# A six-layer transformer kernel on one Trainium2 core: closing tile, first steps of a layer and opening tile in another order, and the exponential's table loaded at another place

## The chip, the cores and the metric

One Trainium2 chip, one of its NeuronCores. The core has five engines that run their own instruction streams and meet at semaphores: TensorE (PE, matmuls and transposes), VectorE (DVE), ScalarE (ACT), GpSimd (POOL) and SyncE (SP, which issues the DMAs here). The metric is the device time of one execution in microseconds; less is better.

## The reference, cut to what matters

```python
x = x + layernorm(attn(layernorm(x)))          # x: (2, 1024, 128)
h = layernorm(x)
for i in range(6):                             # DEPTH
    h = attn_layer(h, Wqkv[i], ...) + h        # 16 heads of 64, window 32
    h = ffn_layer(h, ln_g[i], ...) + h
x = x + layernorm(h)

def attn_layer(x, Wqkv, qs, ksc, Wo):
    q, k, v = split(x @ Wqkv)                  # 128 -> 3 * 1024
    q, k = l2norm(q) * qs, l2norm(k) * ksc     # per head
    q, k = rotary(q), rotary(k)
    sim = q @ k.T * 8, masked to 32 keys back
    return (softmax(sim) @ v) @ Wo

def ffn_layer(x, g, bln, W1, b1, W2, b2):
    xn = layernorm(x) * g + bln
    a, gate = split(xn @ W1 + b1)              # 128 -> 2 * 341
    return a * gelu(gate) @ W2 + b2
```

In each layer half of the channels are taken from the row before (a token shift) ahead of both parts. All is float32.

## The kernel before

The 2048 rows are 16 tiles of 128 rows. All activations stay in the core's memory, channels on the partitions (`xA` ahead of attention, `xB` between attention and feed-forward). A first, small attention fills the first 180 us; then come six layers. A layer has 16 attention tiles, one by one, and a feed-forward part over four groups (s = 0 to 3) of four tiles each. The code of layer 0 and of layer 5 is written out; layers 1 to 4 are one loop over the layer on each engine. Within a layer the tiles 0 and 1 are written out, tiles 2 to 13 are a loop of two tiles per turn, then tiles 14 and 15. Tile 0 is called *opening*, tile 15 *closing*. The order of the work on each engine is written out by hand; semaphores alone hold the engines together.

One tile t of attention does this, while tile t+1 is being prepared:

- Preparation: ScalarE copies the input (`copy_input`), VectorE makes its rest (`input_rest`), TensorE projects six blocks of 512 columns (`project` x = 0 to 5; x = 0, 1, 2, 4 are queries and keys, x = 3, 5 values). For each of the four query and key blocks ScalarE squares (`square`, L519), VectorE reduces the squares and multiplies by the rotary tables (`rotary`, L808 to L818), and GpSimd does the rotation's rest (`rotate`: a power L329, a sum L331, a product L334 that gives `w_nat`). TensorE transposes `w_nat` (`transpose_heads`, L1208), ScalarE copies it to `qT` or `kT` (`heads_T`, L541), and values go out by `values` (L526), which lets the SP queue store them in the layout that the last matmul wants (`move_values`).
- Attention for heads 0 to 7 and then 8 to 15: `scores` (L1158, the mask, and L1167), `maxima` on VectorE (L765), `exps` on ScalarE (L503, two groups of four heads), `transpose_probs` (L1174), `probs_out` (L512), `weigh_values` (L1187), `heads_out` on VectorE (L773, L775, which gives `o_nat`), `transpose_out` (L1214), `heads_out_T` (L532), `project_out` (L1222) and `residual` (L782, L783).

The closing tile has no tile t+1 to prepare; in its place the feed-forward part begins: `shifted(s)` on ScalarE (L464, L465), `transpose_in(s)` on TensorE (L1271), `norm_stats(s)` on VectorE (L924 to L930), a power on GpSimd (L405), `norm(s)` on VectorE (L938), `transpose_normed(s)` (L1278), `normed_T(s)` on ScalarE (L644). For each group s there are three chunks i: `gate_up(s, i)` (L1290, L1292), `gate(s, i)` on ScalarE (the Gelu, L653), `hidden(s, i)` on VectorE (L949); then `down(s)` (L1303) and `output(s)` on VectorE (L957, L959). `split` and `rest` make the next layer's weights ready meanwhile. From s = 2 on, the next layer's tile 0 is prepared between the groups, in numbered parts `start(..., part)`.

Exp and Gelu are in different tables of ScalarE: a load of the Gelu table stands ahead of each layer's first Gelu, one of the exponential's table ahead of the first `exps` of layers 1 to 5.

The lines that two of the prediction's steps hang on are these (VectorE's closing tile, ScalarE's tile):

```python
maxima(t, p, 0)
if closing:
    norm_stats(0)
if not opening:
    heads_out(t - 1, 1 - p, 1)
...
exps(t, p, 0, 0)
if not closing:
    square(t + 1, 0)
```

Of the kernel before, what the change touches and what calls it, by code (L numbers as in the profile page):

```python
# [34 lines left out]
def build(nc, x, Wa, ba, Wp, bp, Wqkv, Wo, scales, W1, W2, par, rope, ident, identb, mask, select, out):  # L35
# [3 lines left out]
    with ctx:  # L39
# [87 lines left out]
        veps = sb("veps", [P, TILES])  # L127
        rstd = sb("rstd", [P, TILES])
# [294 lines left out]
        def _(eng):  # L423
# [155 lines left out]
            def start(t0, part):  # L579
# [7 lines left out]
                if part == 2:  # L587
                    square(t0, 2, True)
                    values(t0, 0, 0)
                if part == 3:  # L590
                    heads_T(t0, 0, 0, 6)
                    square(t0, 3, True)
                    heads_T(t0, 0, 1, 4)
                    values(t0, 0, 1)

            def layer(l, last):
                t0 = l * TILES

                def tile(t, n, p, opening, closing):
                    if closing:  # L600
                        shifted(l, 0)
                        shifted(l, 1)
                    exps(t, p, 0, 0)
                    if not closing:
                        square(t + 1, 0)
                    heads_T(t, p, 2, 6 if opening else 4)
                    if not opening:
                        heads_out_T(t - 1, 1, 6)
                    exps(t, p, 0, 1)
                    if not closing:  # L610
                        square(t + 1, 1)
                    heads_T(t, p, 3, 4)
                    if not closing and not (isinstance(n, int) and n == TILES - 2):
                        copy_input(n + 2, p)
                    probs_out(t, 0, 0, 6)
                    if not closing:
                        square(t + 1, 2)
                    probs_out(t, 0, 1, 4)
# [42 lines left out]
                for s in range(SUPERS):  # L661
# [5 lines left out]
                    gate(s, 1)  # L667
                    if s == 0 and not last:
# [14 lines left out]
                if not last:  # L683
                    start(t0 + TILES, 3)
            for part in range(4):
# [12 lines left out]
        def _(eng):  # L698
# [217 lines left out]
            def layer(l, last):  # L916
# [45 lines left out]
                def tile(t, n, p, opening, closing):  # L962
                    maxima(t, p, 0)
                    if closing:
                        norm_stats(0)
# [4 lines left out]
                    if closing:  # L970
                        norm(0)
# [26 lines left out]
                for s in range(SUPERS):  # L998
                    hidden(s, 1)
# [4 lines left out]
                    elif not last:  # L1004
                        start(l + 1, 3)
# [36 lines left out]
        def _(eng):  # L1042
# [202 lines left out]
            def start(l, part):  # L1245
# [7 lines left out]
                if part == 1:  # L1253
                    project(t0, 0, 2, True)
                    project(t0, 0, 3, True)
                if part == 2:
                    transpose_heads(t0, 0, 6)
                    project(t0, 0, 4, True)
                if part == 3:
# [3 lines left out]
            def layer(l, last):  # L1263
# [42 lines left out]
                def tile(t, n, p, opening, closing):  # L1306
# [19 lines left out]
                    if closing:  # L1326
                        transpose_in(1)
                    else:
                        project(t + 1, 1 - p, 1)
                    eng.wait_ge(tp_free, t * 4 + (2 if opening else 3))  # L1330
                    transpose_heads(t, 3, 4)
                    if opening:
                        eng.wait_ge(tp_free, t * 4 + 3)
                    else:
                        eng.wait_ge(ot_evac, t * 2)
                    transpose_probs(t, 0, 0, 6)
# [138 lines left out]
```

## Time and profile before

| | us |
|---|---|
| median of 3 runs | 2061.19 (2056.7 to 2067.75) |
| the profiled execution | 2066.27 |
| its span, first to last instruction | 2064.5 |
| TensorE busy | 1912.5 (93%) |
| GpSimd busy | 1669.6 (81%) |
| ScalarE busy | 1596.2 (77%) |
| VectorE busy | 1556.0 (75%) |
| mean granted TensorE clock | 0.972 |

Busy time is the time in which an engine has an instruction in work. The granted clock is a share of TensorE's full speed: 1.00 is 2.4 GHz, 0.50 is 1.2 GHz. The time outside the span, 1.8 us, is start and end of the program.

### The profile page before, as it was taken

The page shows a single profiled execution, that of the slowest core. Times are in us where ns is not written, and L with a number is a line of the kernel's source. Part 1 is how long each engine was busy: PE and PEld are TensorE (multiplying, and loading weights), DVE is VectorE, ACT ScalarE, POOL GpSimd, SP SyncE. Part 2 cuts the span into 40 slices and gives each one's busy share as a digit, 9 for nine tenths or more (in the row PEclk, how much of TensorE's full clock was granted, in tenths as well). Part 3 has the DMA queues.
Part 4 walks back from the last instruction along what each step waited for, and adds up shares of the span by engine and source line. Part 5 has one row for each costly group of instructions (what it writes and reads, how often), then busy time and mean ns, then how long its engine had stood idle before and what let it go on. Part 6 is the DMA issues. An engine that isn't in the chain of part 4 may idle for free.

```text
span 2064.5 us, 67226 instructions
## 1 busy us (share of the span) xinstructions
PE 1912.5 (93%) x22192; PEld 1452.2 (70%) x22192; DVE 1556.0 (75%) x4021; ACT 1596.2 (77%) x5607; POOL 1669.6 (81%) x1264
## 2 busy tenths in 40 slices
PE   6996999988999988999988999988999989999997
PEld 4664777765777764777764777774777774777773
DVE  5786888866888866888866788865788876788876
ACT  5874888875888874888874888884888875888873
POOL 3335999976999975999975999984999985999971
PEclk8997999999999999999999999999999999999999
DMA  3001211111211112122112111212211111111210
GB/s 117 14 12 49 60 48 46 46 42 60 60 48 46 46 42 61 48 50 56 46 36 67 48 46 49 56 35 63 56 46 46 46 47 35 50 46 46 50 41 21
DMA packets 44547, 99.42 MB, mean 48 GB/s; under 512 B 7345, under 2 KB 24209, under 8 KB 43505
## 3 DMA queue, kind: packets, MB, share of 16 engines
q1 hardware_dynamic: 44400, 97.59, 18.1%
q8 instruction: 78, 1.28, 0.3%
q14 instruction: 69, 0.56, 0.1%
HBM read 19.59 MB, written 1.05 MB: 10 GB/s over the span
## 4 chain that ended last, share of the span: by engine, by line
PE 81%; ACT 7%; issue 6%; DVE 4%; POOL 1%; DMA 0%; SPq 0%; DVEq 0%; ACTq 0%; POOLq 0%
PE bank L1174 10%; PE bank L1187 9%; PE bank L1222 8%; PE bank L1201 8%; PE bank L1167 7%; PE bank L1203 6%; PE bank L1202 6%; PE bank L1208 6%; PE bank L1158 3%; ACT kT L541 3%; PE bank L1292 3%; PE bank L1290 3%; PE bank L1303 2%; PE bank L1214 2%; ACT prob L503 2%
## 5 line engine op out<-in xcount | busy, mean ns | idle before, releaser
L329 POOL TENSOR_TENSOR rn<-n2c,half_neg 128x8 f32<-128x8 f32 x384 | 636.5, 1658 | 117.9 <-DVE n2c L815 116.8
L503 ACT ACTIVATE prob<-bank,nmax 128x96 f32<-128x96 f32 x1536 | 502.6, 352 | 134.9 <-DVE nmax L765 134.7
L331 POOL TENSOR_TENSOR tsum<-tc_,ts_ 128x512 f32<-128x512 f32 x384 | 489.7, 1275 | 0.0
L334 POOL TENSOR_TENSOR w_nat<-tsum,rn 128x512 f32<-128x512 f32 x384 | 400.9, 1044 | 37.7 <-POOL tsum L331 15.1
L808 DVE TENSOR_REDUCE n<-nat 128x8 f32<-128x512 f32 x384 | 262.2, 683 | 158.4 <-ACT nat L519 143.6
L503 ACT ACTIVATION_READ_ACCUMULATOR prob<-bank,nmax 128x1 f32 x1536 | 333.0, 217 | 0.0
L765 DVE TENSOR_REDUCE nmax<-bank 128x4 f32<-128x384 f32 x384 | 196.2, 552 | 162.4 <-PE bank L1167 162.4
L1201 PE MATMUL bank<-w_hi,xs 128*128 128x512 f32 x576 | 277.9, 482 | 20.1 <-DVE ts_ L818 17.5
L1174 PE MATMUL bank<-idf,prob 128*96 128x128 f32 x1536 | 247.3, 285 | 53.0 <-ACT kT L541 29.1
L512 ACT ACTIVATE pT<-bank 96x512 f32<-96x512 f32 x384 | 230.6, 600 | 74.7 <-PE bank L1174 72.5
L818 DVE TENSOR_TENSOR ts_<-bank,ropeL 128x256 f32<-128x256 f32 x768 | 285.9, 414 | 0.0
L519 ACT ACTIVATE nat<-bank 128x512 f32<-128x512 f32 x384 | 232.9, 607 | 42.3 <-PE bank L1203 33.6
L811 DVE TENSOR_TENSOR tc_<-bank,ropeL 128x512 f32<-128x512 f32 x384 | 261.2, 680 | 0.0
L1174 PEld LDWEIGHTS bank<-idf,prob 128*96 128x96 f32 x1536 | 160.0, 128 | 116.5 <-ACT kT L541 81.0
L1208 PE MATMUL bank<-idf,w_nat 128*128 128x128 f32 x1536 | 236.8, 277 | 3.4 <-POOL w_nat L334 3.2
L1208 PEld LDWEIGHTS bank<-idf,w_nat 128*128 128x128 f32 x1536 | 181.5, 141 | 77.6 <-issue 29.1
L1203 PE MATMUL bank<-w_hi,xs_lo 128*128 128x512 f32 x576 | 229.4, 398 | 0.0
L1202 PE MATMUL bank<-w_lo,xs 128*128 128x512 f32 x576 | 229.4, 398 | 0.0
L1187 PE MATMUL bank<-vspace,pT 96*64 96x64 f32 x6144 | 221.2, 225 | 0.0
L1187 PEld LDWEIGHTS bank<-vspace,pT 96*64 96x64 f32 x6144 | 194.7, 138 | 31.4 <-issue 20.7
L1222 PE MATMUL bank<-oT,wo 128*128 128x128 f32 x1536 | 207.5, 279 | 4.1 <-ACT oT L532 4.1
L1222 PEld LDWEIGHTS bank<-oT,wo 128*128 128x128 f32 x1536 | 190.0, 195 | 6.0 <-ACT oT L532 5.5
(124 smaller groups left out, 3328.1 us busy)
## 6 DMA issues: line engine op xcount, KB each, us to landing
vspace<-v_nat SPq DMA_DIRECT2D x96, 384.0 KB, 4.0
vspace<-v_nat SPq DMA_DIRECT2D x96, 256.0 KB, 3.4
vspace<-v_nat SPq DMA_DIRECT2D x95, 128.0 KB, 2.2
nat<-w_qkv SPq DMA_DIRECT2D x5, 1536.0 KB, 7.9
wo<-w_o SPq DMA_DIRECT2D x6, 512.0 KB, 4.0
w<-w SPq DMA_DIRECT2D x6, 341.0 KB, 3.1
shared<-w_qkv SPq DMA_DIRECT2D x1, 1536.0 KB, 9.9
w<-w SPq DMA_DIRECT2D x6, 192.0 KB, 3.2
```

The lines of the kernel that those rows point to most:

```text
L329: nc.gpsimd.tensor_tensor(rn[:, r, :], n2c[:, r, :], half_neg[:, 0:8], ALU.pow).then_inc(pool_step, 1)
L331: nc.gpsimd.tensor_tensor(tsum[:, r, :], tc_[:, r, :], ts_[:, r, :], ALU.add).then_inc(pool_step, 1)
L334: nc.gpsimd.tensor_tensor(w_nat[:, r, :].rearrange("p (h d) -> p h d", d=D), tsum[:, r, :].rearrange("p (h d) -> p h d", d=D), rn[:, r, :] ...
L503: last = nc.scalar.activation(prob[:, 4 * b + i, :], SB[b][:, i * SPAN:(i + 1) * SPAN], ACT.Exp, bias=nmax[:, p, 8 * G + 4 * b + i:8 * G + ...
L818: last = nc.vector.tensor_tensor(ts_[:, r, :].rearrange(heads3, d=D)[:, :, lo:lo + D // 2], pj[:, :].rearrange(heads3, d=D)[:, :, hi:hi + ...
L1174: last = nc.tensor.transpose(RING[at][0:SPAN, i * P:(i + 1) * P], prob[:, 4 * b + i, :], idf[:, :])
L1187: last = nc.tensor.matmul(OB[qs, a:a + D], pT[:, 4 * b + i, qs], vw[:, p, half, head * D:(head + 1) * D], start=True, stop=True, skip_grou ...
L1201: nc.tensor.matmul(PJ[x % 2][:, :], xs[:, p, :], hi, start=True, stop=False)
L1202: nc.tensor.matmul(PJ[x % 2][:, :], xs[:, p, :], rest, start=False, stop=False)
L1203: nc.tensor.matmul(PJ[x % 2][:, :], xs_lo[:, p, :], hi, start=False, stop=True).then_inc(pj_ready, 1)
L1208: last = nc.tensor.transpose(RING[at][:, i * P:(i + 1) * P], w_nat[:, j % 2, i * P:(i + 1) * P], idf[:, :])
L1222: last = nc.tensor.matmul(YB[:, 0:P], wo[:, 4 * G + i, :], oT[:, G, i * P:(i + 1) * P], start=G == 0 and i == 0, stop=G == 1 and i == 3)
```

## The change

ScalarE: in the closing tile `shifted(1)` moves behind `heads_out_T`, and the two `probs_out` of heads 0 to 7 move ahead of `heads_T` 3. In the opening tile `square(t + 1, 0)` moves ahead of the first `exps`. In the feed-forward part the value copy of tile 0 moves behind `gate(3, 1)`, and a one-column Exp is put behind the last Gelu, ahead of the last part of `start`. VectorE: in the closing tile `norm_stats(0)` moves behind `heads_out` and `residual`; rotary 2 of the next layer's tile 0 moves ahead of `hidden(3, 1)`. TensorE: in the closing tile `transpose_probs` of heads 0 to 7 come ahead of `transpose_heads` 3 (banks 4 and 6 change places), and `project_out(t - 1, 1)` comes ahead of `transpose_probs` 1,0; `project` 3 of the next layer's tile 0 moves behind `gate_up(3, 1)`.

```diff
@@ ScalarE, def start(t0, part)
                 if part == 2:
                     square(t0, 2, True)
+                if part == 3:
                     values(t0, 0, 0)
-                if part == 3:
+                if part == 4:
                     heads_T(t0, 0, 0, 6)
@@ ScalarE, def tile
                     if closing:
                         shifted(l, 0)
-                        shifted(l, 1)
+                    if opening:
+                        square(t + 1, 0)
                     exps(t, p, 0, 0)
-                    if not closing:
+                    if not opening and not closing:
                         square(t + 1, 0)
                     heads_T(t, p, 2, 6 if opening else 4)
                     if not opening:
                         heads_out_T(t - 1, 1, 6)
+                    if closing:
+                        shifted(l, 1)
                     exps(t, p, 0, 1)
                     if not closing:
                         square(t + 1, 1)
+                    if closing:
+                        probs_out(t, 0, 0, 4)
+                        probs_out(t, 0, 1, 6)
                     heads_T(t, p, 3, 4)
...
-                    probs_out(t, 0, 0, 6)
                     if not closing:
+                        probs_out(t, 0, 0, 6)
                         square(t + 1, 2)
-                    probs_out(t, 0, 1, 4)
+                        probs_out(t, 0, 1, 4)
@@ ScalarE, def layer
                     gate(s, 1)
+                    if s == 3 and not last:
+                        start(t0 + TILES, 3)
...
                 if not last:
-                    start(t0 + TILES, 3)
+
+                    nc.scalar.activation(one_exp[:, :], half_neg[:, 0:1], ACT.Exp)
+                    start(t0 + TILES, 4)
@@ VectorE, def tile
                     maxima(t, p, 0)
-                    if closing:
-                        norm_stats(0)
                     if not opening:
                         heads_out(t - 1, 1 - p, 1)
                         if not (isinstance(n, int) and n == 1):
                             residual(t - 2, n - 2)
                     if closing:
+                        norm_stats(0)
                         norm(0)
                         norm_stats(1)
@@ VectorE, feed-forward
                 for s in range(SUPERS):
+                    if s == 3 and not last:
+                        start(l + 1, 3)
                     hidden(s, 1)
                     if s + 2 < SUPERS:
                         norm_stats(s + 2)
                     elif s == 2 and not last:
                         start(l + 1, 0)
-                    elif not last:
-                        start(l + 1, 3)
@@ TensorE, def start
                 if part == 1:
                     project(t0, 0, 2, True)
+                if part == 2:
                     project(t0, 0, 3, True)
-                if part == 2:
+                if part == 3:
                     transpose_heads(t0, 0, 6)
                     project(t0, 0, 4, True)
-                if part == 3:
+                if part == 4:
                     transpose_heads(t0, 1, 4)
                     project(t0, 0, 5, True)
@@ TensorE, def tile
                     if closing:
+
                         transpose_in(1)
+                        eng.wait_ge(tp_free, t * 4 + 3)
+                        transpose_probs(t, 0, 0, 4)
+                        eng.wait_ge(ot_evac, t * 2)
+                        transpose_probs(t, 0, 1, 6)
+                        eng.wait_ge(pt_evac, t * 4 + 1)
+                        transpose_heads(t, 3, 4)
...
                     if closing:
+                        eng.wait_ge(pt_evac, t * 4 + 2)
                         transpose_normed(0)
+                        weigh_values(t, p, 0)
+                        project_out(t - 1, 1)
+                        eng.wait_ge(tp_free, t * 4 + 4)
+                        transpose_probs(t, 1, 0, 4)
@@ TensorE, feed-forward
                     if s + 2 < SUPERS:
                         transpose_in(s + 2)
+                    elif s == 3 and not last:
+                        start(l + 1, 2)
...
                     gate_up(s, 2)
                     if s == 3 and not last:
-                        start(l + 1, 2)
+                        start(l + 1, 3)
...
                 if not last:
-                    start(l + 1, 3)
+                    start(l + 1, 4)
```

## Rows read from the trace of the kernel before

**Rows 1.** The page, part 1: busy us, share of the span, instructions.

```profile
PE 1912.5 (93%) x22192; PEld 1452.2 (70%) x22192; DVE 1556.0 (75%) x4021; ACT 1596.2 (77%) x5607; POOL 1669.6 (81%) x1264
```

**Rows 2.** Windows, steady stretches: window, us, busy us (instructions), granted clock, DMA share, GB/s.

```profile
206.35:438.86 232.51, 224.81 (x2960) 182.19 (x2957) 190.06 (x474) 201.72 (x713) 225.01 (x173) 1.00 0.21 51
...
sum 1394.75, PE 1349.58 PEld 1092.87 DVE 1139.68 ACT 1209.96 POOL 1341.75; mean PE 224.93 PEld 182.14 DVE 189.95 ACT 201.66 POOL 223.63
```

**Rows 3.** Windows, closings of layers 0 and 2, and the sum of six.

```profile
438.86:457.45 18.59, 15.57 (x171) 12.32 (x171) 8.24 (x31) 12.07 (x38) 11.29 (x6) 0.91 0.01 2
...
1062.98:1080.36 17.38, 14.09 (x171) 10.96 (x171) 8.24 (x31) 11.82 (x38) 11.29 (x7) 1.00 0.00 1
...
sum 112.85, PE 93.95 PEld 74.93 DVE 49.46 ACT 71.92 POOL 58.45; mean PE 15.66 PEld 12.49 DVE 8.24 ACT 11.99 POOL 9.74
```

**Rows 4.** Windows, feed-forward parts of layers 0 to 4: their sum.

```profile
sum 133.67, PE 132.98 PEld 65.91 DVE 87.00 ACT 75.01 POOL 45.47; mean PE 26.60 PEld 13.18 DVE 17.40 ACT 15.00 POOL 9.09
```

**Rows 5.** Windows, openings of layers 0, 1, 2 and 5, and the sum of six.

```profile
180.20:206.35 26.15, 20.88 (x175) 14.23 (x175) 19.03 (x45) 15.82 (x53) 25.34 (x20) 0.84 0.31 96
484.24:516.22 31.98, 25.88 (x191) 16.42 (x190) 21.42 (x54) 18.47 (x56) 26.75 (x21) 0.95 0.31 97
795.11:830.33 35.22, 26.98 (x191) 17.04 (x190) 21.40 (x54) 18.83 (x56) 27.33 (x21) 0.90 0.29 89
...
1735.45:1765.84 30.39, 25.92 (x192) 16.42 (x191) 21.40 (x54) 18.58 (x56) 26.90 (x21) 0.94 0.17 45
sum 196.02, PE 153.78 PEld 98.79 DVE 126.02 ACT 109.33 POOL 160.96; mean PE 25.63 PEld 16.47 DVE 21.00 ACT 18.22 POOL 26.83
```

**Rows 6.** Timeline of TensorE in the closings: start, us, what [idle before <-releaser].

```profile
439.86 0.63 PE L1214 MATMUL bank<-idf,o_nat 128*128 128x128 f32 x4 [2.92 <-DVE o_nat L775]
...
444.66 0.49 PE L1158 MATMUL bank<-msk,idb 128*128 128x384 bf16 x2
...
1067.49 0.49 PE L1158 MATMUL bank<-msk,idb 128*128 128x384 bf16 x2
```

**Rows 7.** Timeline of ScalarE, first copy of the closing tile of layer 0.

```profile
434.46 0.62 ACT L464 ACTIVATE shared<-xB 64x512 f32<-64x512 f32 x1
```

**Rows 8.** Timeline of TensorE, end of the feed-forward part and opening, layer 1.

```profile
487.56 0.47 PE L1201 MATMUL bank<-w_hi,xs 128*128 128x512 f32 x1 [1.52 <-DVE ts_ L818]
...
493.14 0.47 PE L1201 MATMUL bank<-w_hi,xs 128*128 128x512 f32 x1 [0.78 <-DVE ts_ L818]
...
499.20 0.50 PE L1201 MATMUL bank<-w_hi,xs 128*128 128x512 f32 x1
```

**Rows 9.** Timeline of ScalarE, opening tiles of layers 0, 1 and 2.

```profile
192.97 0.34 ACT L503 ACTIVATE prob<-bank,nmax 128x96 f32<-128x96 f32 x1 [2.08 <-DVE nmax L765]
...
194.25 0.61 ACT L519 ACTIVATE nat<-bank 128x512 f32<-128x512 f32 x1
...
200.24 0.34 ACT L503 ACTIVATE prob<-bank,nmax 128x96 f32<-128x96 f32 x1 [0.56 <-DVE nmax L765]
...
499.99 1.28 ACT L503 ACT_TABLE_LOAD   x1 [1.57 <-DVE nmax L765]
...
502.56 0.61 ACT L519 ACTIVATE nat<-bank 128x512 f32<-128x512 f32 x1
...
808.58 0.60 ACT L526 ACTIVATE v_nat<-bank 128x512 f32<-128x512 f32 x1
812.72 1.28 ACT L503 ACT_TABLE_LOAD   x1 [3.54 <-issue]
...
816.13 0.60 ACT L519 ACTIVATE nat<-bank 128x512 f32<-128x512 f32 x1 [0.72 <-issue]
```

**Rows 10.** Timeline of GpSimd, last product of tile 0 and first power of tile 1, layer 1.

```profile
499.33 1.04 POOL L334 TENSOR_TENSOR w_nat<-tsum,rn 128x512 f32<-128x512 f32 x1
504.75 1.65 POOL L329 TENSOR_TENSOR rn<-n2c,half_neg 128x8 f32<-128x8 f32 x1 [4.38 <-DVE n2c L815]
```

**Rows 11.** Windows, a stretch of the opening tile of layer 4.

```profile
1441.32:1451.32 10.00, 6.42 (x47) 4.51 (x48) 4.67 (x12) 5.94 (x20) 5.80 (x5) 0.50 0.49 175
```

More of the change, by code:

```diff
@@ L127, in build @@
         veps = sb("veps", [P, TILES])
+        one_exp = sb("one_exp", [P, 1])
         rstd = sb("rstd", [P, TILES])
@@ L683, in layer @@
                 if not last:
-                    start(t0 + TILES, 3)
-            for part in range(4):
+                    nc.scalar.activation(one_exp[:, :], half_neg[:, 0:1], ACT.Exp)
+                    start(t0 + TILES, 4)
+            for part in range(5):
                 start(0, part)
@@ L1327, in tile @@
                         transpose_in(1)
+                        eng.wait_ge(tp_free, t * 4 + 3)
[4 more added lines that the diff above has]
+                        transpose_heads(t, 3, 4)
                     else:
                         project(t + 1, 1 - p, 1)
[L1330 to L1336, printed above, removed]
-                    if not closing:
+                        eng.wait_ge(tp_free, t * 4 + (2 if opening else 3))
+                        transpose_heads(t, 3, 4)
+                        if opening:
+                            eng.wait_ge(tp_free, t * 4 + 3)
+                        else:
+                            eng.wait_ge(ot_evac, t * 2)
+                        transpose_probs(t, 0, 0, 6)
                         project(t + 1, 1 - p, 2)
-                    eng.wait_ge(tp_free, t * 4 + 4)
-                    transpose_probs(t, 0, 1, 4)
+                        eng.wait_ge(tp_free, t * 4 + 4)
+                        transpose_probs(t, 0, 1, 4)
                     scores(t, n, p, 1)
@@ L1344, in tile @@
                         project(t + 1, 1 - p, 3)
-                    eng.wait_ge(pt_evac, t * 4 + 1)
                     if closing:
+                        eng.wait_ge(pt_evac, t * 4 + 2)
                         transpose_normed(0)
+                        weigh_values(t, p, 0)
+                        project_out(t - 1, 1)
+                        eng.wait_ge(tp_free, t * 4 + 4)
+                        transpose_probs(t, 1, 0, 4)
                     else:
+                        eng.wait_ge(pt_evac, t * 4 + 1)
                         transpose_heads(t + 1, 0, 6)
-                    weigh_values(t, p, 0)
-                    eng.wait_ge(pt_evac, t * 4 + 2)
-                    transpose_probs(t, 1, 0, 4)
-                    if not opening:
-                        project_out(t - 1, 1)
+                        weigh_values(t, p, 0)
+                        eng.wait_ge(pt_evac, t * 4 + 2)
+                        transpose_probs(t, 1, 0, 4)
+                        if not opening:
+                            project_out(t - 1, 1)
                     if closing:
@@ L1400, in layer @@
                 if not last:
-                    start(l + 1, 3)
-            for part in range(4):
+                    start(l + 1, 4)
+            for part in range(5):
                 start(0, part)
```

## The prediction

> **What bounds the kernel now.** I read the page first. TensorE is busy 93% of the span, which looks like the bound, but GpSimd is at 81% and ScalarE at 77% [rows 1]. So I cut each layer with the windows view into four stretches whose ends I took from the timelines. (1) Steady: from the first scores of tile 1 to the end of the last `w_nat` multiply of tile 15. All six are 232.5 us on average; GpSimd is busy 225.01 of 232.51 us in the first, at full granted clock: that stretch runs at the rotation's pace, and no edit is in it [rows 2]. (2) Closing: from that multiply to the last half of `project_out`. It takes 17.38 us in layer 2, where the granted clock stayed at 1.00 (the higher level, 2.4 GHz), 18.59 us in layer 0, where it was 0.91, and 112.85 us in all six [rows 3]; the five others so lost 8.6 us against layer 2, 1.7 each. (3) Feed-forward: from there to the first rotation of the next layer, 133.67 us in five, 26.73 each; TensorE is busy 132.98 of it, so it is TensorE's [rows 4]. (4) Opening: from that rotation to the first scores of tile 1. 26.15 us in layer 0, 31.98 in layer 1, 35.22 in layer 2, 30.39 in layer 5, 196.02 in all, so 72.28 for layers 3 and 4 [rows 5]. The reader is to see that layer 0 does this work, without a table load and without a feed-forward part beside it, in 4 to 10 us less than the others. Closing and opening are the only places where an edit can pay.
>
> **Closing tile.** TensorE waits 2.92 us for `o_nat`, because VectorE does `norm_stats(0)` ahead of `heads_out`; behind it stand the output transpose, the projection and all else of the tile [rows 6]. The swap on VectorE takes this wait away: the o_nat multiply, which needed only `weigh_values`, comes about 2.9 us earlier. But that isn't the gain, since ScalarE ends last next. Its new order from 434.46 [rows 7] is `shifted(0)` (two copies, 1.30), four exps (1.28, the distance of the rows at 192.97 and 194.25 in layer 0), two head copies (1.0), `shifted(1)` (1.30), four exps (1.28): 440.6. Then three handoffs of about 0.15, a transpose of probabilities (0.45), one of keys (0.60), the copy between them hidden, `heads_T` 3 (0.60) and the wait of `scores`: second scores at 443.0, which is 4.15 us after the last multiply at 438.86. Before, it is at 444.66 (5.80) in layer 0, where the clock had fallen, and 4.51 (1067.49 less 1062.98) in layer 2, where it hadn't [rows 6]. From there to the end the same chain follows. So a closing at full clock should take 17.38 - 0.37 = 17.0. What the clock does is the unknown. Before, TensorE's 2.92 us of idleness is followed by a fallen clock in layer 0 and, by the sum of times, in the four others too. In the new order TensorE still idles some 2.9 us, in pieces of at most 1.3, while ScalarE works. If the clock stays up everywhere: 112.85 - 6 x 17.0 = 10.9 us gained; if it falls as before: 6 x 0.37 = 2.2 us. I take the middle, 6.5.
>
> **End of the feed-forward part.** `project` 3 goes behind `gate_up(3,1)`, and rotary 2 ahead of `hidden(3,1)`. TensorE's waits of 1.52 us (for rotary 1) and 0.78 us (for rotary 2) [rows 8] are covered: the first by 1.7 us of gate_up, the second because rotary 2 no longer waits for hidden(3,1), and starts when GpSimd has finished rotation 0. `down(3)` then waits some 0.25 us for hidden(3,2), which is behind rotary 2. So all behind it comes 1.52 + 0.78 - 0.25 = 2.05 us earlier: the first scores, and `project(t+1,0)` from 499.20 to 497.15. The new load and the one-column Exp stand behind the last Gelu, where ScalarE waits for TensorE anyway; 1.28 us plus some 0.3 end about as square 3 becomes ready. Without that cover they would cost 1.6 per layer in layers 1 to 5. The value copy triggers the SP queue's three stores of values 2 us earlier; nothing asks for them before `weigh_values`, behind the second scores. The window to the first rotation keeps its 26.7.
>
> **Opening tile, layers 1 and 5.** Before, `square(t+1,0)` starts at 502.56: behind the scores' maxima, the load (1.28) and four exps [rows 9]. First in line, it starts when its projection ends, 497.15 + 1.0 = 498.15, 4.4 us earlier. GpSimd then is free only at 499.33 + 1.04 = 500.4, so rotation (1,0) starts at 500.5 instead of 504.75: 4.25 us [rows 10]. How fast the rest follows layer 0 tells: from its first exps at 192.97 to the third group at 200.24 are 7.27 us, with square and all, and from there to its end (180.20 + 26.15 = 206.35) 6.11 [rows 5, 9]. 498.15 + 7.27 + 6.11 = 511.5, instead of 484.24 + 31.98 = 516.22: a window of 27.3, gain 4.7. Layer 5 goes from 30.39 to 27.3: 3.1. Layer 0 has no load to save and its GpSimd is busy 25.34 of 26.15 us: square waits for its projection there, exps behind it: 0, within 0.3.
>
> The table load as the row has it: 1.28 us, and from its start to the square 2.57 us, all of it load and exps [rows 9]. The Trainium skill, page ScalarE: Activation LUTs, section What ACT_TABLE_LOAD costs, gives some 1283 ns plus a drain of 1380; by it another 1.4 us would leave the path in layers 1 and 5, 2.8 in sum. The trace has no room for that drain here, and I don't count it.
>
> **Opening tile, layers 2 to 4.** Here the table load isn't what ends last. The layers' loop jumps back, and ScalarE waits for nothing that the profile shows ("issue") for 3.54 us before the load and 0.72 us before the square [rows 9]; layers 1 and 5, entered without the jump, have no such wait. In layer 2 the last value copy ends at 808.58 + 0.60 = 809.18, the second wait 6.95 us later at 816.13, and the window 14.2 us after that. The load passes within the 6.95 and saves nothing. I expect both waits to follow the value copy as before, 2.05 us earlier, and the square (0.5) to be done by the second: 2.6 us each, 7.8 in three. The Trainium skill, Runtime: NRT & Kernel Launch, section Instruction fetch mechanics, speaks against the change here: a taken branch to outside the two resident pages forces a fetch before work goes on, whatever the order behind it. The trace agrees, with the 3.54.
> Bounds: nothing but the square (0.5 each, 1.5), if the second fetch comes no earlier; and above, the 14.2 shrinks to layer 0's 206.35 - 194.25 = 12.1, if TensorE's clock stays up: 6.3 more in three. I take the same 14.2, since TensorE still stands behind ScalarE's waits there.
>
> **Sum.** 6.5 (closings) + 4.7 + 3.1 + 7.8 = 22.1 us. The profiled execution took 2066.27 us, 1.8 around its span of 2064.5, and is 5.1 above the median of the three runs. It becomes 2044.2; the median 2061.2 becomes 2039.
>
> **Rivals.**
> - Handed to the clock and the fetch: closings 2.2, layers 2 to 4 1.5, and layers 1 and 5 lose 1.3 each to a fall of the clock like today's (7.8 - 2.6 = 5.2). 8.9 us, 2052. For it: the clock fell in most closings, and TensorE's idleness is only cut up. Against: the waits of 2 us and more go. 0.2.
> - The clock stays up: 10.9 + 7.8 + 7.8 + 6.3 = 32.8, 2028.4. For it: layer 2's closing, which kept its clock behind the same wait. 0.17.
> - The load isn't moved: a load still stands ahead of the opening's exps. Layers 1 and 5 lose 1.28 each, 2042. Against: both ways into the loop now end on Exp. 0.05.
> - Slower: thin work of TensorE in the closing leaves it at the lower level (1.2 GHz) into the feed-forward, which is TensorE's. Layer 4 has such a stretch, 10 us at 0.50, 6.42 busy [rows 11]. Matmuls take double there, so 7.4 us of busy time at that level in each of six layers eats the 22.1; 15 us would make 2084. Against: TensorE is busy 132.98 of 133.67 us in the five feed-forward windows, and before them its idleness is no longer than today. 0.05.
> - The forecast: 0.53.
>
> **How the numbers follow.** The time is the forecast's, 2039; its own range 2032 to 2047. The range goes to both neighbours, 2026 to 2054. A change within 0.5% (10.3 us) is about what can't be told from none. Faster takes the forecast, the upper case, the unmoved load and a third of the lowest gain: 0.82; same 0.13; slower 0.05.
>
> **What would show it.** Steady windows stay at 232.5, the feed-forward at 26.7. Closings 17 to 18.5, without the wait for o_nat of 2.9. Five loads behind the last Gelu, none before the exps. The two TensorE waits of 1.52 and 0.78 gone. GpSimd's gap before rotation (1,0) from 4.4 to 0.2 in layer 1, in layers 2 to 4 still over 3, behind "issue". Openings 27.3 in layers 1 and 5, 33 in 2 to 4. I am wrong if closings lengthen, if the second fetch moves otherwise than the value copy, or if the granted clock falls in the feed-forward.

## The result, and the profile after

The changed kernel takes 2033.2 us (median of 4 runs, 2031.17 to 2034.99), the kernel before 2063.99 in the same comparison: ratio 0.9859, 95% interval 0.9834 to 0.9884. That is 30.8 us less, where the forecast was 22. The profiled execution took 2031.44 us, with a span of 2029.6 and a mean granted clock of 0.982 (before: 2064.5 and 0.972). Of all runs below one was slow, 2165.6 us at a clock of 0.842 in e11_before_unrolled; it is among the four of that kernel's median (2045.97, or 2045.21 without it), and its ratio leaves it out.

The same windows, laid by the same ends, for the changed kernel. First the closings (layers 0 and 5, sum of six), as in [rows 3]:

```profile
435.28:451.84 16.56, 12.93 (x159) 9.55 (x159) 7.01 (x27) 11.65 (x37) 11.30 (x7) 1.00 0.00 1
...
1966.10:1982.65 16.55, 12.93 (x158) 9.54 (x158) 7.01 (x27) 11.65 (x37) 2.03 (x2) 1.00 0.01 1
sum 99.61, PE 77.55 PEld 57.30 DVE 42.09 ACT 69.89 POOL 58.48; mean PE 12.93 PEld 9.55 DVE 7.01 ACT 11.65 POOL 9.75
```

Then the openings, as in [rows 5]:

```profile
176.89:203.05 26.16, 20.99 (x174) 14.39 (x175) 19.00 (x46) 15.93 (x53) 25.59 (x20) 0.80 0.30 96
478.64:505.93 27.29, 24.29 (x191) 15.23 (x190) 21.91 (x54) 18.46 (x57) 26.40 (x21) 1.00 0.37 114
781.88:813.50 31.62, 25.74 (x192) 16.27 (x191) 21.93 (x54) 18.58 (x57) 27.43 (x21) 0.95 0.32 99
1089.44:1122.40 32.96, 26.88 (x192) 17.08 (x191) 22.57 (x52) 18.58 (x57) 27.60 (x21) 0.90 0.31 95
1398.34:1431.17 32.83, 25.87 (x192) 16.30 (x190) 22.57 (x52) 18.57 (x57) 27.44 (x21) 0.90 0.32 95
1707.10:1734.15 27.05, 24.06 (x191) 15.30 (x190) 21.91 (x54) 18.46 (x57) 26.34 (x21) 1.00 0.18 50
sum 177.91, PE 147.84 PEld 94.57 DVE 129.89 ACT 108.57 POOL 160.80; mean PE 24.64 PEld 15.76 DVE 21.65 ACT 18.10 POOL 26.80
```

And the sums of the six steady stretches and the five feed-forward parts, as in [rows 2, 4]:

```profile
sum 1394.58, PE 1357.97 PEld 1100.99 DVE 1145.31 ACT 1210.16 POOL 1342.81; mean PE 226.33 PEld 183.50 DVE 190.88 ACT 201.69 POOL 223.80
```

```profile
sum 133.66, PE 133.00 PEld 65.92 DVE 87.01 ACT 75.01 POOL 45.40; mean PE 26.60 PEld 13.18 DVE 17.40 ACT 15.00 POOL 9.08
```

Against before, the closings give 112.85 - 99.61 = 13.2 us and the openings 196.02 - 177.91 = 18.1; steady stretches and feed-forward parts give 0.2 and 0.0. The sum, 31.5, is the difference of the medians within their spread. The two profiled spans are 34.9 apart, because the first rotation starts at 176.89 instead of 180.20; that start lies between 176.7 and 183.0 in the kernels below, with no order to it, and nothing ahead of it is changed. So I compare kernels by windows first, and by medians second. The windows come from one profiled execution of each kernel, and openings wander too: with the same opening code the six take 196.02, 193.40 and 194.03 us (the kernel before, e1_closing, e2_swap_alone), or 177.91, 178.39 and 180.34 (the changed kernel, e8_old_norm_stats, e10_swap_in_changed). With the clock at 1.00 closings of the same code agree within 0.1 us in the sum of six.

Now the single steps. TensorE in the closing of layer 0; the row at 439.03 is the start of the second scores:

```profile
435.73 0.66 PE L1283 MATMUL bank<-idf,shared 128*128 128x128 f32 x4 [1.01 <-ACT shared L466]
...
439.03 0.50 PE L1169 MATMUL bank<-msk,idb 128*128 128x384 bf16 x2 [0.73 <-ACT kT L542]
```

The wait of 2.92 us for `o_nat` [rows 6] is gone; what waits now waits for ScalarE, 1.01 us for `shifted(1)`, 0.42 us for the exps and 0.73 us for the last key copy. The second scores start 3.75 us after the last product instead of 5.80.

TensorE at the end of the feed-forward part of layer 0, `project` 3 and `down(3)`:

```profile
481.96 0.47 PE L1212 MATMUL bank<-w_hi,xs 128*128 128x512 f32 x1
...
486.21 2.84 PE L1315 MATMUL bank<-shared,w 128*128 128x512 f32 x6 [0.28 <-DVE shared L961]
```

Both waits of [rows 8] are gone; in their place `down(3)` waits 0.28 us for the last `hidden`. ScalarE at the same time, with the load at its new place, and then GpSimd at rotation (1,0), which answers to [rows 10]:

```profile
484.49 1.28 ACT L695 ACT_TABLE_LOAD   x1
485.78 0.20 ACT L695 ACTIVATE one_exp<-half_neg 128x1 f32<-128x1 f32 x1
485.89 0.58 ACT L542 ACTIVATE qT<-bank 128x512 f32<-128x512 f32 x1
```

```profile
494.86 1.65 POOL L330 TENSOR_TENSOR rn<-n2c,half_neg 128x8 f32<-128x8 f32 x1 [0.18 <-DVE n2c L827]
```

GpSimd's gap of 4.38 us has shrunk to 0.18. Last, ScalarE at the head of layer 2, behind the jump back of the layers' loop, which answers to [rows 9]:

```profile
793.47 0.60 ACT L527 ACTIVATE v_nat<-bank 128x512 f32<-128x512 f32 x1
797.47 0.60 ACT L520 ACTIVATE nat<-bank 128x512 f32<-128x512 f32 x1 [3.41 <-PE bank L1214]
...
798.28 0.34 ACT L504 ACTIVATE prob<-bank,nmax 128x96 f32<-128x96 f32 x1
...
801.02 0.34 ACT L504 ACTIVATE prob<-bank,nmax 128x96 f32<-128x96 f32 x1 [2.30 <-issue]
```

Both waits are still there. The first is put down to a projection that had ended at 795.83 + 0.39 = 796.22, 1.2 us before ScalarE moved; in layer 3 the same wait, 3.67 us, is put down to nothing ("issue"). The second now comes in the middle of the exps. GpSimd's gap before rotation (1,0), 7.1 to 8.4 us in layers 2 to 4 before, is 1.7 to 2.1 us, as the square now stands ahead of the second wait.

### The profile page after: what moved, and what is told of

Read it like the earlier page. It is cut to its first block, busy times and chain, and to the rows that moved or that the text cites. A ratio compares the mean times of both kernels' runs of the same rounds, so it can differ in the third digit from the quotient of the medians.

```text
span 2029.6 us, 67231 instructions
## 1 busy us (share of the span) xinstructions
PE 1895.1 (93%) x22192; PEld 1435.4 (71%) x22192; DVE 1558.0 (77%) x4021; ACT 1593.5 (79%) x5612; POOL 1670.5 (82%) x1264
## 3 DMA queue, kind: packets, MB, share of 16 engines
q8 instruction: 78, 1.28, 0.3%
## 4 chain that ended last, share of the span: by engine, by line
PE 79%; ACT 8%; issue 6%; DVE 3%; POOL 2%; DMA 0%; ACTq 0%; DVEq 0%; POOLq 0%
PE bank L1185 10%; PE bank L1198 9%; PE bank L1233 8%; PE bank L1212 8%; PE bank L1178 7%; PE bank L1214 6%; PE bank L1213 6%; PE bank L1219 6%; PE bank L1169 3%; ACT kT L542 3%; PE bank L1315 3%; ACT prob L504 2%; PE bank L1304 2%; PE bank L1302 2%; PE bank L1225 2%
```

## The experiments

Eleven kernels, in three groups that each ran beside the kernel before on one chip (its medians there: 2062.38 for the first four, 2061.74 for the next four, 2061.63 for the last three). The windows of each are laid by the same ends as above.

**The closing tile alone.** The kernel before, with the whole closing tile of the change: VectorE's swap, ScalarE's `shifted(1)` and `probs_out` moves, and TensorE's closing branches. The core of it, on VectorE and then on ScalarE:

```diff
                     maxima(t, p, 0)
-                    if closing:
-                        norm_stats(0)
...
                     if closing:
+                        norm_stats(0)
                         norm(0)
...
-                        shifted(l, 1)
...
+                    if closing:
+                        shifted(l, 1)
                     exps(t, p, 0, 1)
...
+                    if closing:
+                        probs_out(t, 0, 0, 4)
+                        probs_out(t, 0, 1, 6)
                     heads_T(t, p, 3, 4)
```

> The kernel before with the closing tile of the changed kernel on ScalarE, VectorE and TensorE, and nothing else of the change. Theory 1 (the closing tile is worth the change's whole gain there, by the shorter ScalarE order and a granted clock that no longer falls): closings of 16.6 us each at clock 1.00, 99.6 in six instead of 112.9, openings as before (26.2, 32.0, 35.2, 36.5, 35.8, 30.4), so 13 us less than before, near 2051. Theory 2 (the clock of the closing depends on what else the change does in the layer): closings between 17 and 18.5, clock below 1.00 in several, at most 8 us less.

Measured: 2053.58 us, ratio 0.9951 (0.9935 to 0.9968). Closings 99.6 us in six, clock 1.00 in each, as in the changed kernel; openings 193.40 in six. Theory 1 holds, theory 2 falls: the closing's gain of 13.2 us in the windows is independent of the rest of the change. The medians show 8.8 us of it (by the interval, 7 to 13); the profiled execution, 2047.08 us, was the fastest of five.

**VectorE's swap alone.** The kernel before with two lines moved on VectorE, and nothing on the two other engines:

```diff
                     maxima(t, p, 0)
-                    if closing:
-                        norm_stats(0)
...
                     if closing:
+                        norm_stats(0)
                         norm(0)
```

> The kernel before with one edit: VectorE does norm_stats(0) behind heads_out and residual; ScalarE and TensorE keep their old order of the closing tile. Theory 1 (this swap is all that the closing needs; the other moves add two copies ahead of the last key copy): the wait for o_nat of 2.9 us goes, the second scores start 2.9 to 3.1 us after the last product instead of 3.75 in the changed kernel, closings of 15.7 to 16.1 us, 17 to 19 us less than before in all. Theory 2 (ScalarE's and TensorE's new orders are what makes the closing short): closings of 17 us or more, or the clock falls as before; at most 8 us less.

Measured: 2047.44 us, ratio 0.9922 (0.9894 to 0.9950). The closing of layer 0 and the sum:

```profile
439.79:455.46 15.67, 12.35 (x155) 9.15 (x155) 7.11 (x27) 11.70 (x38) 11.29 (x7) 1.00 0.01 1
...
sum 94.31, PE 74.12 PEld 54.92 DVE 42.63 ACT 70.14 POOL 58.49; mean PE 12.35 PEld 9.15 DVE 7.10 ACT 11.69 POOL 9.75
```

TensorE in that closing, last probabilities' transpose and second scores:

```profile
442.19 0.64 PE L1173 MATMUL bank<-idf,prob 128*96 128x128 f32 x4 [1.14 <-ACT kT L541]
442.67 0.49 PE L1157 MATMUL bank<-msk,idb 128*128 128x384 bf16 x2
```

The second scores start 442.67 - 439.79 = 2.88 us after the last product, 0.87 earlier than in the changed kernel. So the swap is worth 18.5 us in six closings (14.9 by the medians), and ScalarE's and TensorE's moves cost 5.3 of them: they put two copies of probabilities ahead of the last key copy, which the scores wait for. The moves of these two engines were not tried apart.

**The change without the preload.**

```diff
-                    nc.scalar.activation(one_exp[:, :], half_neg[:, 0:1], ACT.Exp)
```

> The changed kernel without the one-column Exp, so that the exponential's table is loaded ahead of the opening tile's exps again, behind the square. Theory 1 (a load costs its 1.28 us and is hidden where ScalarE waits for its code): openings of layers 1 and 5 of 28.4 to 28.6 instead of 27.3 and 27.05, those of layers 2 to 4 unchanged at 31.6 to 33, 2.6 us more than the changed kernel. Theory 2 (a load costs 2.66 us with its drain): 29.9 in layers 1 and 5. Theory 3 (the square first is worth nothing without the load's move): rotation (1,0) falls back to 504.75 less 484.24, 20.5 us after the first rotation.

Measured: 2037.67 us, ratio 0.9872 (0.9851 to 0.9893). Openings of layers 1 and 5, the sum of six, then ScalarE in layer 1:

```profile
484.53:514.64 30.11, 25.98 (x191) 16.25 (x190) 22.49 (x52) 18.56 (x56) 27.56 (x21) 0.94 0.32 103
...
1716.79:1746.55 29.76, 25.78 (x191) 16.29 (x190) 22.50 (x52) 18.57 (x56) 27.54 (x21) 0.94 0.17 45
sum 184.92, PE 151.57 PEld 96.83 DVE 131.25 ACT 109.45 POOL 163.35; mean PE 25.26 PEld 16.14 DVE 21.88 ACT 18.24 POOL 27.22
```

```profile
499.18 1.28 ACT L504 ACT_TABLE_LOAD   x1
500.48 0.34 ACT L504 ACTIVATE prob<-bank,nmax 128x96 f32<-128x96 f32 x1
```

The opening of layer 1 grew by 30.11 - 27.29 = 2.8 us and that of layer 5 by 2.7; layers 2 to 4 add 1.5 in sum, no more than openings wander by. That is the number of theory 2, but not its mechanism: the load takes 1.28 us and the first exps start at once behind it. TensorE shows the rest, at the second scores:

```profile
506.33 1.56 PE L1176 MATMUL bank<-kT,qT 64*64 64x96 f32 x32
```

The 32 small matmuls take 1.56 us there, and 0.89 us at full clock (the first scores, at 490.78 in the changed kernel): the granted clock is 0.50 in this stretch, and 1.00 all through the opening with the preload. Ahead of it TensorE waits 1.15 us for a query copy, a wait that the changed kernel doesn't have. So the load costs its 1.28 us and, behind this longer idleness of TensorE, some 1.5 us of low clock. My 1.28 was half of it. Theory 3 falls: rotation (1,0) starts 16.2 us after the first, as with the preload. The Trainium skill (ScalarE: Activation LUTs, section What ACT_TABLE_LOAD costs) reckons 2.66 us with a drain; no row here shows this drain, and by the rows the agreement of the sum is chance.

**ScalarE's layers written out.** The changed kernel, one edit on ScalarE:

```diff
-            layers(eng, layer)
+            for l in range(DEPTH):
+                layer(l, l == DEPTH - 1)
```

> The changed kernel with ScalarE's six layers written out instead of a loop over layers 1 to 4; the other engines keep their loop. Theory 1 (the two waits of ScalarE at the head of layers 2 to 4, 3.5 and 2.3 to 3.0 us, are the jump back of the layers' loop): both waits go, openings of layers 2 to 4 fall to 27.3, 15.5 us less than the changed kernel, near 2018. Theory 2 (they come from the transfers of values and weights that fill the DMA engines at that time, whatever the code): 31.6 to 33 remain, no gain.

Measured: 2020.77 us, ratio 0.9794 (0.9775 to 0.9813). Openings of layers 2 to 4, then ScalarE at the head of layer 2:

```profile
785.77:813.66 27.89, 24.43 (x192) 15.29 (x191) 21.93 (x54) 18.46 (x57) 26.42 (x21) 1.00 0.36 112
1089.43:1117.25 27.82, 24.43 (x192) 15.28 (x190) 21.92 (x54) 18.46 (x57) 26.43 (x21) 1.00 0.38 112
1393.02:1420.63 27.61, 24.43 (x192) 15.27 (x190) 21.92 (x54) 18.46 (x57) 26.41 (x21) 1.00 0.36 113
```

```profile
797.36 0.60 ACT L527 ACTIVATE v_nat<-bank 128x512 f32<-128x512 f32 x1
800.41 0.60 ACT L520 ACTIVATE nat<-bank 128x512 f32<-128x512 f32 x1 [2.45 <-PE bank L1215]
800.90 0.34 ACT L504 ACTIVATE prob<-bank,nmax 128x96 f32<-128x96 f32 x1
...
801.85 0.35 ACT L504 ACTIVATE prob<-bank,nmax 128x96 f32<-128x96 f32 x1
```

14.1 us less in three openings, though the same transfers run at the same time (0.36 to 0.38 of the DMA engines). The wait in the middle of the exps is gone, and the first ends with the projection. Theory 1 holds: the waits are the loop's jump. That ScalarE waits for code no row of an engine says, but the profile lists the transfers of instructions. The page's line for the queue that changes with this edit, in the changed kernel and in this one, then the same queue in the changed kernel from 1106.80 to 1107.50:

```profile
q14 instruction: 69, 0.56, 0.1%
```

```profile
q14 instruction: 58, 0.48, 0.1%
```

```profile
q14 instruction: 1, 0.01, 5.3%
```

Only ScalarE's code differs, and eleven such transfers are gone. In the changed kernel one of them stands in each second wait: they end at 799.66, 1107.49 and 1417.19 in layers 2, 3 and 4, and ScalarE goes on 1.36, 1.36 and 1.37 us behind them (801.02, 1108.85, 1418.56). The first waits end 0.72, 0.15 and 0.82 us behind such a transfer. So the waits are very likely for ScalarE's instructions; the rows don't name the engine that a transfer is for. The Trainium skill says the same (Runtime: NRT & Kernel Launch, section Instruction fetch mechanics): a taken branch out of the resident pages forces a fetch; with the jump gone the waits are gone, and so the rule and the runs agree.

**Both together.** The changed kernel with the closing tile of ScalarE and TensorE as before (VectorE's swap stays), and ScalarE's layers written out. On ScalarE:

```diff
+                        shifted(l, 1)
...
-                    if closing:
-                        shifted(l, 1)
...
-                    if closing:
-                        probs_out(t, 0, 0, 4)
-                        probs_out(t, 0, 1, 6)
...
-            layers(eng, layer)
+            for l in range(DEPTH):
+                layer(l, l == DEPTH - 1)
```

> The changed kernel with ScalarE's and TensorE's closing tile as in the kernel before (VectorE's swap stays), and ScalarE's layers written out. Theory (the two gains are at different places and add up): closings of 15.7, 94.3 in six instead of 99.6, openings as in e4_scalar_unrolled (27.2, 27.9, 27.8, 27.6, 27.1), so 5.3 us less than e4_scalar_unrolled, near 2015.5. Rival (a shorter closing is given back in the opening or the clock falls in one of them): 2019 or more.

Measured: 2011.81 us, ratio 0.9758 (0.9739 to 0.9777). Closings 94.23, openings 164.10. The two gains add up; the rival falls.

**All engines but SyncE written out.** The kernel of the last experiment, with the loop's edit on VectorE, TensorE and GpSimd too. GpSimd's lines, then those of each of the two others:

```diff
-            with eng.Fori(0, DEPTH - 1) as l:
-                layer(l, False)
-            layer(DEPTH - 1, True)
+            for l in range(DEPTH):
+                layer(l, l == DEPTH - 1)
...
-            layers(eng, layer)
+            for l in range(DEPTH):
+                layer(l, l == DEPTH - 1)
```

> As e5_swap_unrolled, with the layers of all engines but SyncE written out. Theory 1 (only ScalarE's jump costs; the other engines jump while they would wait anyway): openings of layers 2 to 4 stay at 27.6 to 27.9 or go to the 27.2 of layer 1, at most 2 us less in all. Theory 2 (the 0.4 to 0.7 us that layers 2 to 4 still have over layer 1 are TensorE's or VectorE's jump): they go to 27.2. Theory 3 (more code costs, as each engine must stream it): new waits for nothing in the steady stretch, more than 232.6 us each, slower than e5_swap_unrolled.

Measured: 2010.17 us, ratio 0.9745 (0.9727 to 0.9763), the fastest kernel of this study. Sums of closings and openings:

```profile
sum 94.02, PE 74.17 PEld 54.93 DVE 42.58 ACT 70.15 POOL 58.49; mean PE 12.36 PEld 9.15 DVE 7.10 ACT 11.69 POOL 9.75
```

```profile
sum 161.91, PE 141.81 PEld 90.92 DVE 127.92 ACT 108.23 POOL 158.09; mean PE 23.63 PEld 15.15 DVE 21.32 ACT 18.04 POOL 26.35
```

All six openings are 26.97 to 27.00 us. So the 0.5 to 0.8 us that layers 2 to 4 kept over layer 1 in e5_swap_unrolled were the jumps of the other engines (theory 2); which engine's, was not tried. Against e5_swap_unrolled the openings give 2.2 us, and the steady stretches don't grow (1391.9 in six, 1393.0 there): theory 3 falls. By the medians alone the two kernels can't be told apart.

**The end of the feed-forward part in the old order.** The changed kernel with these lines back:

```diff
                 if part == 2:
                     square(t0, 2, True)
-                if part == 3:
                     values(t0, 0, 0)
...
-                    if s == 3 and not last:
-                        start(l + 1, 3)
                     hidden(s, 1)
+                    if s == 3 and not last:
+                        start(l + 1, 3)
...
                     project(t0, 0, 2, True)
-                if part == 2:
                     project(t0, 0, 3, True)
```

> The changed kernel with the end of the feed-forward part in the old order: project 3 and its value copy ahead of gate_up(3,1) and rotary 2 behind hidden(3,1); the Exp stays behind the last Gelu. Theory 1 (the order there is worth the two waits, 1.52 + 0.78 - 0.25 us): the waits of 1.5 and 0.8 us are back, openings of layers 1 and 5 of 29.3, layers 2 to 4 of 33.6 to 35, 10 us more than the changed kernel in five openings. Theory 2 (GpSimd's rotations, unchanged, bound the opening): at most 0.5 us per opening.

Measured: 2041.82 us, ratio 0.9907 (0.9883 to 0.9930). TensorE's two waits are back, and the opening of layer 1 has grown by 2.01 us, that of layer 5 by 1.90 (28.95), all six by 186.48 - 177.91 = 8.6:

```profile
481.64 0.47 PE L1211 MATMUL bank<-w_hi,xs 128*128 128x512 f32 x1 [1.52 <-DVE ts_ L829]
487.22 0.47 PE L1211 MATMUL bank<-w_hi,xs 128*128 128x512 f32 x1 [0.78 <-DVE ts_ L829]
```

```profile
478.32:507.62 29.30, 24.28 (x192) 15.37 (x190) 21.41 (x54) 18.57 (x57) 26.37 (x21) 1.00 0.34 106
```

Theory 1 holds, by 29.3 as expected.

**The old VectorE order in the new closing tile.** The changed kernel with `norm_stats(0)` ahead of `heads_out` again:

```diff
                     maxima(t, p, 0)
+                    if closing:
+                        norm_stats(0)
...
                     if closing:
-                        norm_stats(0)
                         norm(0)
```

> The changed kernel with VectorE's norm_stats(0) ahead of heads_out and residual again; ScalarE and TensorE keep the new closing tile. Theory 1 (the swap is the closing's gain, and the new ScalarE order without it makes the wait dearer, since the second exps then stand behind heads_out_T and shifted(1)): closings of 19.3 us or more, with TensorE waiting 2.9 us for o_nat and a clock that falls to 0.8 to 0.95, 16 us and more over the changed kernel. Theory 2 (TensorE's idleness in one piece is not what the clock falls by): clock 1.00 in all six closings, though longer.

Measured: one execution, 2055.13 us. Closings of layers 1 and 4 and the sum, then TensorE in the closing of layer 4:

```profile
742.62:764.35 21.73, 18.29 (x170) 13.74 (x170) 8.44 (x31) 13.23 (x39) 11.29 (x7) 0.76 0.00 1
...
1681.07:1700.65 19.58, 14.47 (x171) 10.91 (x171) 8.16 (x31) 12.96 (x39) 11.28 (x6) 1.00 0.00 1
...
sum 122.60, PE 97.77 PEld 74.69 DVE 49.25 ACT 78.76 POOL 58.46; mean PE 16.29 PEld 12.45 DVE 8.21 ACT 13.13 POOL 9.74
```

```profile
1681.98 0.66 PE L1226 MATMUL bank<-idf,o_nat 128*128 128x128 f32 x4 [2.89 <-DVE o_nat L787]
```

With the wait, the clock falls below 1.00 in five closings of six, as before; with the same wait of 2.89 us it stays at 1.00 in layer 4. In the changed kernel and the nine others that have the swap it is 1.00 in every closing of every profile. So theory 1 holds: without the wait the clock never fell, and with it the clock doesn't have to fall. The 23.0 us over the changed kernel are mostly the chain: where the clock stayed up, the closing is 19.58 - 16.64 = 2.9 us longer, near 18 in six; the rest, some 5, is the clock. ScalarE's and TensorE's moves without the swap make the closing worse than the kernel before had it (122.60 against 112.85).

**The square behind the first exps.** The changed kernel with the opening's `square(t + 1, 0)` back in its old place:

```diff
-                    if opening:
-                        square(t + 1, 0)
                     exps(t, p, 0, 0)
-                    if not opening and not closing:
+                    if not closing:
                         square(t + 1, 0)
```

> The changed kernel with the opening tile's square(t+1,0) behind the first exps again; the Exp stays behind the last Gelu. Theory 1 (ScalarE's work in the opening is the same in either order, so only GpSimd's start moves): rotation (1,0) starts 17.5 us after the first instead of 16.2 in layer 1, opening of layer 1 within 0.5 us of 27.3, at most 0.6 us lost per layer there, and 1.5 us in each of layers 2 to 4, where the square would stand behind the second wait for code. 2 to 6 us over the changed kernel in all. Theory 2 (the earlier rotation is the opening's gain): the 4.7 us of layers 1 and 5 shrink by 1.3 us or more each.

Measured: 2037.97 us, ratio 0.9879 (0.9856 to 0.9902). Openings of layers 1 and 3 and the sum:

```profile
483.01:510.42 27.41, 24.52 (x192) 15.16 (x191) 22.75 (x54) 18.55 (x57) 25.57 (x20) 1.00 0.36 114
...
1095.55:1130.71 35.16, 27.12 (x191) 17.27 (x190) 21.91 (x54) 18.87 (x57) 27.36 (x21) 0.85 0.31 89
...
sum 181.97, PE 151.10 PEld 96.17 DVE 130.72 ACT 109.41 POOL 157.70; mean PE 25.18 PEld 16.03 DVE 21.79 ACT 18.24 POOL 26.28
```

Theory 1 holds; rotation (1,0) starts 17.25 us after the first in layer 1. In layers 1 and 5 the order is worth 0.1 and -0.1 us in the opening and 0.3 to 0.4 in the steady stretch behind it; in layers 2 to 4 1.4, 2.2 and 0.2, where the square now stands behind the second wait. These three are of the size by which openings wander between profiles, so the 4.1 us in six are not well clear of noise.

**The swap as the only edit of the closing tile, in the changed kernel.** ScalarE's and TensorE's closing tile is that of before. On TensorE, in core:

```diff
-                        eng.wait_ge(tp_free, t * 4 + 3)
-                        transpose_probs(t, 0, 0, 4)
-                        eng.wait_ge(ot_evac, t * 2)
-                        transpose_probs(t, 0, 1, 6)
-                        eng.wait_ge(pt_evac, t * 4 + 1)
-                        transpose_heads(t, 3, 4)
...
+                    transpose_heads(t, 3, 4)
...
+                    transpose_probs(t, 0, 0, 6)
...
+                    transpose_probs(t, 0, 1, 4)
```

> The changed kernel with ScalarE's and TensorE's closing tile as before, so that VectorE's swap is the only edit of the closing tile. Theory (the other moves cost 0.9 us per closing, whatever the openings are): closings of 15.7 us at clock 1.00, 94.3 in six, 5.3 us less than the changed kernel, near 2028. Rival (what is saved in the closing is waited for in the opening): no less than 2032.

Measured: 2029.52 us, ratio 0.9842 (0.9822 to 0.9862). Closings 94.22 instead of 99.61 (15.66 to 15.73 in each layer), openings 180.34. The closings give 5.4 us, as the theory has it. The median is 3.7 us below 2033.2, between the two theories' numbers. The openings of layers 0 and 3 are 1.6 and 1.0 longer than in the changed kernel's profile, the others within 0.6; but layer 0's has no closing ahead of it, and the five that have one are 0.9 longer in sum. The closing's gain is shown; that it is fully kept in this combination is not.

**The kernel before with ScalarE's layers written out.**

```diff
-            layers(eng, layer)
+            for l in range(DEPTH):
+                layer(l, l == DEPTH - 1)
```

> The kernel before with ScalarE's layers written out and nothing else. Theory 1 (in the old order, too, the two waits of layers 2 to 4 are the layers' jump): openings of layers 2 to 4 fall from 35.2 to 36.5 to what layer 5 (30.4) and layer 1 (32.0) have, 10 to 17 us less than before, near 2049. The load then stands on the path in these layers as well. Theory 2 (the waits follow the value stores and weights in either code): 35 and more remain.

Measured: 2045.97 us, ratio 0.9918 (0.9888 to 0.9948). Openings of layers 2 and 3:

```profile
791.17:820.79 29.62, 24.57 (x192) 15.26 (x190) 22.28 (x54) 18.56 (x56) 25.52 (x20) 1.00 0.34 106
1100.05:1129.71 29.66, 24.58 (x191) 15.26 (x190) 22.27 (x54) 18.57 (x56) 25.53 (x20) 1.00 0.36 106
```

Layer 4 has 30.84. The three openings give 107.50 - 90.12 = 17.4 us: theory 1, and nearly as much as the whole change gets out of all six openings (18.1). The closings, in the old order, bear on e8_old_norm_stats: TensorE waits 2.9 us for `o_nat` in each, and the clock stays at 1.00 in layers 0, 1 and 5 and falls to 0.83, 0.91 and 0.83 in layers 2 to 4. Layer 0:

```profile
439.92:457.27 17.35, 14.06 (x170) 10.95 (x170) 8.25 (x31) 11.82 (x38) 11.28 (x6) 1.00 0.01 2
```

## Why the prediction was right, point by point

- *The size.* 30.8 us measured, 22.1 forecast: the direction and the mechanisms held, two terms were too small. The measured gain lies nearer to the rival in which the clock stays up (32.8 us, given a chance of 0.17) than to the forecast, and the time of 2033.2 is just inside the forecast's own range of 2032 to 2047. Taken from the median of 2061.2 that the forecast started from, 30.8 us less would be 2030.4, outside it.
- *Steady stretches and feed-forward parts stay.* They did, within 0.2 us in the sum of the six and 0.1 in that of the five.
- *Closings, 6.5 us.* 13.2. The mechanism was right, the term was mis-sized: I took the middle between a clock that stays (10.9) and one that falls as before (2.2). It stayed in all six, and a closing took 16.6 us instead of the 17.0 of my walk: the handoffs from the last exps to the second scores took 439.03 less 436.98 = 2.05 us, and I had put 2.4. Also wrong in emphasis: I had ScalarE's new order in the sum as if it were needed; e2_swap_alone shows that the swap without it is better by 0.9 us per closing.
- *End of the feed-forward part, 2.05 us.* 2.01 and 1.90 by e7_old_ffn_order, with `down(3)` waiting 0.28 us instead of my 0.25.
- *Openings of layers 1 and 5, 4.7 and 3.1.* 4.7 and 3.3; both windows within 0.3 us of the predicted 27.3. Layer 0 as a model for the others held. But of the causes the load was worth twice its 1.28 us, through the clock (e3_no_preload), and the square's place next to nothing there (e9_square_behind). GpSimd's start moved by 4.3 us, and it doesn't set the end: in e3_no_preload the rotation starts as early as in the changed kernel and the opening is 2.8 us longer, and in the changed kernel the second product of tile 1 is done at 502.93 and TensorE takes it up at 503.87. That layer 1's window came out at 27.3 with the load mis-sized by 1.5 us is in part luck.
- *Openings of layers 2 to 4, 7.8.* 3.6 + 3.5 + 3.0 = 10.1. The waits did move with the value copy, roughly: in layer 2 the second ended 801.02 - 794.07 = 6.95 us behind it, as before, in layers 3 and 4 7.2 and 8.0 us (8.2 and 7.6 before). Behind the second wait I had put 14.2 - 0.5 = 13.7 us; it was 12.5, 13.5 and 12.6. The wait now falls among the exps, and the low clock is shorter (0.90 to 0.95 over the window, 0.86 to 0.90 before); how the two share the gain isn't shown. The sign I gave of GpSimd's gap, still over 3 us there, was wrong: it is 1.7 to 2.1.
- *The load moves.* Yes, five loads behind the last Gelu, none ahead of exps.
- *The slower rival.* No sign of it: the feed-forward windows have a granted clock of 1.00, and so do the closings.

What the parts are worth, each undone in the changed kernel, in window time: the order at the feed-forward's end 8.6 us, the preload 7.0, the square's place 4.1, VectorE's swap 23.0 (with the new closing order of the two others; 18.5 with the old one), and ScalarE's and TensorE's closing order -5.3. The three of the openings sum to 19.7, and the openings gained 18.1; each of them has the wander of openings in it, some 2 us in six.

## What to carry to other kernels

Cut the span into stretches with fixed ends and compare these, not only the medians: that separates 2 us from a start that wanders by 6. Where a long loop body jumps back, look at the first instructions of each engine behind the jump in every turn, and try the loop written out on the engine that is late: it took two lines here and gave 14 to 17 us in the windows. And when several engines' orders are changed for one wait, run the smallest edit by itself: here one of three engines' edits was better alone.

## What the runs showed that I had not expected

- The granted clock can double the price of a stall. A table load of 1.28 us on the path cost 2.8 us, as the matmuls that come after ran at 0.50 (32 scores in 1.56 us instead of 0.89). It doesn't always: in e1_closing, e2_swap_alone and e11_before_unrolled the load stands on the path of layer 5's opening as before, the clock stayed at 1.00, and the window took 28.8 us instead of 30.39.
- The same wait of 2.9 us on TensorE was followed by a fall in 13 of 18 closings and by none in 5 (layer 4 of e8_old_norm_stats, layer 2 of the kernel before, layers 0, 1 and 5 of e11_before_unrolled). What decides between them the rows don't say, and it stays open.
- Writing the layers out on four engines cost next to nothing: the steady stretches took 1391.9 us in six, and 1394.6 with the loops; the five feed-forward parts took 134.0 instead of 133.7.
